# Decoder layer on one core: the up biases of the expert network move from products of their own into the last row of the up weights

## The chip, the cores and the metric

The kernel runs on one core of a Trainium2 chip. The metric is the device time of one execution in microseconds (us). The engines are called PE (TensorE, the matmuls), DVE (VectorE), ACT (ScalarE), POOL (GpSimd) and SP (SyncE, which here only issues transfers).

## What is computed

A decoder layer with three parts, each followed by a residual sum and a layer norm without gain or offset: self attention with circulant projections, cross attention to a context, and a mixture of 8 experts of which each token takes two, plus one shared expert. There are 16 batches of 128 tokens with 128 features. The change lies in the third part:

```
def _layernorm(x, axis=-1, eps=1e-05):
    m = jnp.mean(x, axis=axis, keepdims=True)
    v = jnp.var(x, axis=axis, keepdims=True)
    return (x - m) / jnp.sqrt(v + eps)
...
    x = _layernorm(x + _L0_xattn_ref(x, ctx_1024, ...), axis=-1)
    x = _layernorm(x + _L0_ffn_ref(x, ...), axis=-1)
...
        scores = jax.nn.softmax(xt @ gate_w.T, axis=-1)
...
            h = swiglu((xt @ ew1 + eb1) * (xt @ ew3 + eb3))
            return (acc + ce[:, None] * (h @ ew2 + eb2), None)
...
    shared = swiglu((xt @ sw1 + sb1) * (xt @ sw3 + sb3)) @ sw2 + sb2
```

The up weights `w1` and `w3` are 128 x 512 for each expert, the down weights `w2` 256 x 128. The input of the third part, called X2 in the kernel, is the output of a layer norm, so the 128 features of each of its rows sum to zero.

## The kernel before, in words

All engines run programs that are written out by hand and tied together by semaphores. The first two parts run in slots n = -20 to 72. There are four slots to a batch (`U = 4`); slot n holds attention step n of PE, ACT and DVE, and beside it the steps k = 1 to 8 of the chains of one to three earlier batches (`chain_steps`). Slots 0 to 63 begin on PE between 40 and 222 us. In step k = 1 and k = 7 of a chain DVE forms the statistics of a layer norm, POOL the reciprocal root (`root`, L612 and L614), and DVE then writes the normed rows X1 (L995) or X2 (L1004). POOL also adds a bias row before and after (X1B L652, XB L669), multiplies `hq_x` (L655), halves the down weights (L679, `HALVE_SLOTS`), and scatters the rows of X2 to their experts' places in DRAM (`xs`, L634), from slot 41 on. SP issues every load of weights, in slots given by the tables `BIAS_SLOTS`, `UP_SLOTS` and `DOWN_SLOTS`, between the loads of the attention parts, in program order: what stands ahead in SP's queue delays what stands behind. The up weights of experts 6 and 7 are loaded last, in slots 67 and 68, since their place holds other data until then.

From slot 66 on follow the tiles of the third part. Two groups of four batches take the shared expert in pieces between slots 25 and 63 (`shared`). All else is 47 tiles of 128 rows (m = 0 to 46): 8 of the shared expert, then 39 (`NR`) that are loaded from `xs` and take one expert each, whose number PE loads into a register (L1520). Step m of PE transposes the hidden rows `hid` of tile m-2 and the input rows of tile m+1 into pO (L1492, L1494), which ACT copies to `XH` (L852); it makes the two up products of tile m into pS and pT (L1501), and the down product of tile m-2 into pM (L1512). ACT copies pS (L858), DVE multiplies it with pT (L1071), clips it (L1073, L1074), ACT takes a tanh (L855), and DVE forms the gate and `hid` (L1076, L1079). ACT weights pM (L868) and POOL scatters it to `ys` (L712). Where PE waits for `hid` of tile m-2, a step is late by what DVE is late.

Each bias is added by a product of its own: three bf16 parts of all bias rows stand in the rows of `bias3`, nine rows of 128, and `bias_rows` picks three of them (L1502 into pS and pT, L1514 into pM). The three parts are made on POOL in slot 24 and pass through DRAM. The shared expert's early pieces add their biases on ACT and DVE instead, by column (`b1_col`, `b3_col`).

The tiles 8 to 23 come from rows that groups 0 to 2 have scattered. The last group's rows are scattered by POOL between the tiles (`LAST_SCATTER`), and SP waits for all of these scatters before it loads the rows of tile 24, whose transpose stands in step 23. Between tiles 5 and 17 DVE also works out the routing of the last group and the table of tiles (`LAST_ROUTING`, `LAST_TILES`).

Of the kernel before, what the change touches and what calls it, by code (L numbers as in the profile page):

```python
# [14 lines left out]
P = 128  # L15
B = 16
D = 128
# [20 lines left out]
BROWS = ((E + 1) * I2 // P, (E + 1) * I2 // P, (E + 1) * D // P)  # L38
# [8 lines left out]
BIAS_SLOTS = {7: 0, 11: 1, 15: 2}  # L47
# [6 lines left out]
XW = D + 2  # L54
# [7 lines left out]
UP_SLOTS = {**{15 + 4 * e: e for e in range(E - 2)}, 67: E - 2, 68: E - 1}  # L62
# [6 lines left out]
def decoder_layer(nc, x, ctx_1024, wq_c, wq_b, wk_c, wk_b, wv_c, wv_b, wo_c, wo_b, w_sim, b_sim, W_qv, b_qv,  # L69
# [3 lines left out]
    bias_scr = nc.dram_tensor("bias_scr", (3, sum(BROWS), P), BF16)  # L73
# [5 lines left out]
    with ctx:  # L79
# [13 lines left out]
        bias_rows = sb("bias_rows", [P, 3, P], BF16)  # L93
# [19 lines left out]
        gw_sb = sb("gw_sb", [E, D])  # L113
        gwT = sb("gwT", [P, E])
# [7 lines left out]
        bias_f = sb("bias_f", [sum(BROWS), P])  # L122
        bparts = sb("bparts", [sum(BROWS), 3, P], BF16)
        bias3 = sb("bias3", [P, (E + 1) * I2], BF16)
# [4 lines left out]
        X2T = sb("X2T", [P, 2, P])  # L129
        XT = sb("XT", [P, 2, G4 * P])  # L130
# [81 lines left out]
        XH = sb("XH", [P, 2, 3 * P])  # L212
# [6 lines left out]
        hidT = [hid[:].rearrange("p k n -> p (k n)"), W1[:, (E - 2) * I2:(E - 1) * I2]]  # L219
        b1_col, b3_col = sb("b1_col", [P, 2, 2]), sb("b3_col", [P, 2, 2])  # L220
        x2_of = [W[:, (E - 1) * I2:E * I2] for W in (W1, W3)]
        lin_g, lin_l = XH[:].rearrange("p k n -> p (k n)")[:, 0:G4 * P], PT[:, 3, :]
# [28 lines left out]
        s_bias3 = sem("s_bias3")  # L251
        s_w_shared, s_w_up, s_w_last, s_w_down = (sem(n) for n in ("s_w_shared", "s_w_up", "s_w_last", "s_w_down"))
        s_bcol = sem("s_bcol")
# [125 lines left out]
        def _(sp):  # L379
# [83 lines left out]
            def up_weights(e, done):  # L463
                a, c = (w1[e], w3[e]) if e < E else (sw1, sw3)
                sp.dma_start(W1[:, e * I2:(e + 1) * I2], a).then_inc(done, 16)
                sp.dma_start(W3[:, e * I2:(e + 1) * I2], c).then_inc(done, 16)
# [13 lines left out]
            for n in range(FIRST_SLOT, LAST_SLOT + 1):  # L480
# [16 lines left out]
                if n in BIAS_SLOTS:  # L497
                    k = BIAS_SLOTS[n]
                    routed, shared = ((b1, sb1), (b3, sb3), (b2, sb2))[k]
                    row = sum(BROWS[:k])  # L500
# [3 lines left out]
                if n == 21:  # L504
                    for to, src in ((b1_col, sb1), (b3_col, sb3)):
                        sp.dma_start(to[:], src.rearrange("(c p l) -> p c l", c=2, l=2)).then_inc(s_bcol, 16)
# [1104 lines left out]
```

## Time and profile before

| | |
|---|---|
| median of 3 runs | 418.36 us (418.06 to 418.45) |
| the profiled execution | 419.23 us, span 417.5 us |
| PE busy | 347.8 us (83% of the span) |
| DVE busy | 282.4 us (68%) |
| POOL busy | 195.5 us (47%) |
| ACT busy | 175.2 us (42%) |
| mean granted clock of PE | 0.956 |
| transfers | 39.56 MB |

The span is what the trace shows; the execution's own time has 1.7 us around it. Busy shares are means over a program with stages of different kinds, so they don't say which engine sets the end of a stage.

### The profile page before, as it was taken

Reading aid. Unit: us, or ns where it says so; the run is one execution under the profiler, and the core shown is the slowest. Engines: PE = TensorE matmul, PEld = TensorE weight load, DVE = VectorE, ACT = ScalarE, POOL = GpSimd, SP = SyncE. Lnnn points to the kernel's source line nnn. Section 1 sums busy time; section 2 is a strip of 40 time slices with the busy share of each in tenths; the row PEclk is TensorE's granted clock in tenths of the full one; section 3 lists DMA queues with packets and bytes.
Section 4 is the critical chain, followed back from the end, with each engine's and each line's share of the span. In section 5 each row is a group of like instructions: output and inputs, shape, how many; then the busy total and the mean of one; then the engine's idle time right before and its main releaser. Section 6 shows DMA issues by size and latency. Waiting matters only on the chain.

```text
span 417.5 us, 8518 instructions
## 1 busy us (share of the span) xinstructions
PE 347.8 (83%) x2415; PEld 224.0 (54%) x2415; DVE 282.4 (68%) x834; ACT 175.2 (42%) x498; POOL 195.5 (47%) x377
## 2 busy tenths in 40 slices
PE   2637887887998987878978699899999999999790
PEld 1223465665765666556657455455456555555450
DVE  3345477776669887888886866788866666666232
ACT  2122344443443452435452154345555555555313
POOL 9700022224213258753275534346888665656223
PEclk9999999998888999989998699999999999999897
DMA  4774644766726533220002100111322111110063
GB/s 98 172 207 123 196 143 117 209 197 175 207 75 206 156 110 91 64 74 23 23 28 72 63 19 26 40 32 52 90 61 64 54 44 46 45 40 19 27 203 100
DMA packets 53197, 39.56 MB, mean 95 GB/s; under 512 B 7623, under 2 KB 46632, under 8 KB 53147
## 3 DMA queue, kind: packets, MB, share of 16 engines
q1 hardware_dynamic: 50881, 34.33, 29.8%
q0 software_dynamic: 2272, 4.69, 3.4%
q8 instruction: 22, 0.36, 0.4%
q14 instruction: 22, 0.18, 0.1%
HBM read 26.05 MB, written 12.69 MB: 93 GB/s over the span
## 4 chain that ended last, share of the span: by engine, by line
PE 50%; DVE 19%; issue 8%; DMA 7%; POOL 7%; SPq 6%; ACT 2%; ACTq 0%; POOLq 0%; DVEq 0%
PE pT L1501 9%; PE pS L1501 9%; PE pM L1512 5%; DVE negmax L934 3%; PE pO L1492 3%; PE pM L1307 2%; DVE inv_den L950 2%; PE pT L1502 2%; PE pS L1502 2%; PE pT L1478 2%; POOL rstd L614 2%; POOL xs L634 2%; PE pO L1344 2%; PE pT L1331 2%; PE pS L1321 2%
## 5 line engine op out<-in xcount | busy, mean ns | idle before, releaser
L712 POOL DMA_INDIRECT ys<-sim_rhs,row_dest x39 | 40.5, 1038 | 36.7 <-ACT sim_rhs L868 32.8
L766 ACT ACTIVATE PT<-pT 128x512 f32<-128x512 f32 x64 | 38.0, 593 | 36.5 <-PE pT L1331 36.1
L1501 PE MATMUL pT<-W,XH 128*128 (+1 forms) x94 | 50.5, 619 | 0.0
L934 DVE TENSOR_REDUCE negmax<-pS 128x4 f32<-128x512 f32 x64 | 43.4, 679 | 9.0 <-PE pS L1321 8.7
L1501 PE MATMUL pS<-W,XH 128*128 (+1 forms) x94 | 49.0, 604 | 0.0
L612 POOL TENSOR_SCALAR vareps<-meanvar 128x1 f32<-128x1 f32 x32 | 8.5, 264 | 86.6 <-DVE meanvar L963 86.3
L1321 PE MATMUL pS<-Kdiag,Qst 128*128 128x512 f32 x64 | 41.5, 655 | 4.9 <-DMA Kdiag<-parts_scr 4.1
L1071 DVE TENSOR_TENSOR PT<-pT,PT 128x512 f32<-128x512 f32 x47 | 32.4, 690 | 19.4 <-PE pT L1502 16.3
L852 ACT COPY XH<-pO 128x384 f32<-128x384 f32 x47 | 22.5, 479 | 46.6 <-PE pO L1494 39.9
L1512 PEld LDWEIGHTS pM<-W,XH 128*128 128x128 f32 x188 | 28.5, 194 | 18.1 <-issue 14.4
L634 POOL DMA_INDIRECT xs<-X,slot x32 | 33.5, 1048 | 7.5 <-issue 5.2
L1331 PE MATMUL pT<-Qdiag,Kst 128*128 128x512 f32 x64 | 30.8, 482 | 2.6 <-DMA Qdiag<-maxT 2.2
L1512 PE MATMUL pM<-W,XH 128*128 (+1 forms) x188 | 29.4, 279 | 1.3 <-ACT XH L852 1.3
L655 POOL TENSOR_TENSOR hq_x<-X1T,hqT 128x128 f32<-128x128 f32 x16 | 7.3, 456 | 49.0 <-ACT hqT L787 49.0
L1076 DVE SCALAR_TENSOR_TENSOR Vz<-Vz,XT 128x256 f32<-128x256 f32 x47 | 20.1, 427 | 14.1 <-ACT Vz L855 12.5
L858 ACT COPY PT<-pS 128x512 f32<-128x512 f32 x47 | 27.2, 580 | 2.4 <-PE pS L1502 2.2
L855 ACT ACTIVATE Vz<-XT 128x256 f32<-128x256 f32 x47 | 19.6, 417 | 19.4 <-DVE XT L1073 17.2
L1344 PE MATMUL pO<-PT,Vz 128*32 128x128 f32 x512 | 27.6, 289 | 0.0
L1348 PE MATMUL pO<-PT,head_ones 128*32 128x128 f32 x512 | 26.5, 280 | 0.0
L1492 PEld LDWEIGHTS pO<-ident,hid 128*128 128x128 f32 x94 | 12.2, 142 | 23.3 <-issue 16.7
L1492 PE MATMUL pO<-ident,hid 128*128 128x128 f32 x94 | 18.4, 277 | 4.5 <-issue 1.7
L1478 PE MATMUL pT<-W 128*128 128x512 f32 x32 | 21.0, 743 | 0.7 <-DVE XH L1043 0.7
(264 smaller groups left out, 823.6 us busy)
## 6 DMA issues: line engine op xcount, KB each, us to landing
parts_scr<-qk_hi SPq DMA_DIRECT2D x16, 256.0 KB, 3.1
W<-in_L_ffn_w SPq DMA_DIRECT2D x16, 256.0 KB, 4.0
Qst<-parts_scr SPq DMA_DIRECT2D x32, 96.0 KB
Kdiag<-parts_scr SPq DMA_DIRECT2D x64, 48.0 KB
Kst<-parts_scr SPq DMA_DIRECT2D x32, 96.0 KB
Qdiag<-parts_scr SPq DMA_DIRECT2D x64, 48.0 KB
sim_add<-xs SPq DMA_DIRECT2D x39, 65.0 KB
parts_scr<-qk_lo SPq DMA_DIRECT2D x8, 256.0 KB, 3.4
```

Of the source, the lines that this page charges most:

```text
L634: pool.indirect_dma_start(xs.ap(), bass.IndirectOffsetOnAxis(ap=slot[:, k, b:b + 1], axis=0), X2[:, b, :], None).then_inc(scat_sem(g), 16)
L712: pool.indirect_dma_start(ys.ap(), bass.IndirectOffsetOnAxis(ap=row_dest[:, k:k + 1], axis=0), YO[:, i % RING, :], None).then_inc(s_ysc[i ...
L766: act.activation(PT[:, u % 3, :], pT[:, 0, :], ACT.Exp, scale=SCALE).then_inc(p_sb, 1)
L934: dve.tensor_reduce(out=negmax[:, b % 2, HG * j:HG * (j + 1)], in_=pS[:, u % 2, :].rearrange("p (g k) -> p g k", g=HG), axis=AX.X, op=ALU.max,
L1071: dve.tensor_tensor(prod[:, p, :], pT[:, p, :], up1[:, p, :], ALU.mult).then_inc(prod_sb, 1)
L1321: pe.matmul(pS[:, u % 2, :], Qst[:, (b // 2) % 2, j, (b % 2) * P:(b % 2 + 1) * P], Kdiag[:, b % 2, j, :, :], start=True, stop=True).then_i ...
L1331: pe.matmul(pT[:, 0, :], Kst[:, (b // 2) % 2, j, (b % 2) * P:(b % 2 + 1) * P], Qdiag[:, b % 2, j, :, :], start=True, stop=True).then_inc(s ...
L1344: pe.matmul(pO[32 * hg:32 * hg + 32, 0:P], Vz[:, b % 2, hg, j, :], PT[:, u % 3, hg * P:(hg + 1) * P], start=(j == 0), stop=(j == U - 1), s ...
L1478: pe.matmul(pT[:, 1, :], (W1, W3)[step % 2][:, first:first + 2 * P - step // 2:2], x2_of[g], start=True, stop=True).then_inc(f_ps, 1)
L1492: mm = pe.transpose(pO[:, k * P:(k + 1) * P], hid[:, p, k * P:(k + 1) * P], ident[:])
L1501: pe.matmul(bank, XH[:, 1 - p, 2 * P:3 * P], W[:, bass.ds(e_up * I2, I2)], start=True, stop=False)
L1512: pe.matmul(pM[:, 0:D], XH[:, p, k * P:(k + 1) * P], W2[:, bass.ds(e_y * I + k * D, D)], start=(k == 0), stop=False)
```

## The change

Because each row of X2 sums to zero, its feature 0 is minus the sum of the others. So x @ W is the sum over the features 1 to 127 of x_d (W_d - W_0), which needs only 127 rows, and the 128th row of the contraction is free: X2 gets a column of ones behind its features, the transposes take columns 1 to 128 of it, and the bias is the last row of the weights. What the diff does:

- For each of the nine experts SP now issues four loads in place of two: rows 1 to 126 of each up weight to 126 partitions, and row 0 broadcast to 128 partitions (`first_rows_of`). Row 127 and the bias of all experts come in eight loads in slot 11 (`up_biases`). The slots are 13 for the shared expert and 21 + 5e for expert e, and each waits until the subtractions of the one before are done (`w_less`).
- POOL subtracts the broadcast row from each up weight, 127 x 512, 18 in all, in the third and fourth slot behind each load (`LESS_SLOTS`: 16, 17, 24, 25, 29, 30, 34, 35, 39, 40, 44, 45, 49, 50, 54, 55, 59, 60).
- The two bias products of each tile's up products go. The bias product of the down product stays, with three partitions in place of 128, and moves ahead of the second up product; the down product moves behind it.
- The gate weights get the same treatment by one small subtraction on DVE; the bias parts of the down product are made of 9 rows instead of 81 and no longer pass through DRAM; POOL's clearing of `bias3` and the making of `bias_rows` go.
- The shared expert's early pieces need no bias on ACT and DVE; some buffers that lay in the weights get their own place, so that experts 6 and 7 load in slots 51 and 56.
- The rows of `xs` have 131 elements instead of 130.

```
-UP_SLOTS = {**{15 + 4 * e: e for e in range(E - 2)}, 67: E - 2, 68: E - 1}
+UP_SLOTS = {13: E, **{21 + 5 * e: e for e in range(E)}}
+LESS_SLOTS = {n + 3 + k: (e, k) for n, e in UP_SLOTS.items() for k in range(2)}
...
+                i = LESS_ORDER[e]
+                if i:
+                    sp.wait_ge(w_less, 2 * i)
+                for k, (W, w) in enumerate(((W1, w1 if e < E else sw1), (W3, w3 if e < E else sw3))):
+                    first = e * D * I2 if e < E else 0
+                    sp.dma_start(W[0:P - 2, e * I2:(e + 1) * I2],
+                                 bass.AP(w.tensor, first + I2, [[I2, P - 2], [1, I2]])).then_inc(s_w_up, 16)
+                    sp.dma_start(first_rows_of[:, k, :], bass.AP(w.tensor, first, [[0, P], [1, I2]])).then_inc(s_w_up, 16)
...
+                if n in LESS_SLOTS:
+
+                    e, k = LESS_SLOTS[n]
+                    here = (W1, W3)[k][0:P - 1, e * I2:(e + 1) * I2]
+                    pool.wait_ge(s_w_up, 64 * (LESS_ORDER[e] + 1))
+                    pool.wait_ge(s_w_bias, 128)
+                    pool.tensor_tensor(here, here, first_rows_of[0:P - 1, k, :], ALU.subtract).then_inc(w_less, 1)
...
-                    pe.matmul(bank, XH[:, 1 - p, 2 * P:3 * P], W[:, bass.ds(e_up * I2, I2)], start=True, stop=False)
-                    pe.matmul(bank, bias_rows[:, k, :], bias3[:, bass.ds(e_up * I2, I2)], start=False,
+                    pe.matmul(bank, XH[:, 1 - p, 2 * P:3 * P], W[:, bass.ds(e_up * I2, I2)], start=True,
                               stop=True).then_inc(done, 1)
...
+                if y:
+
+                    if m >= 3:
+                        pe.wait_ge(y_sb, m - 2)
+                    pe.matmul(pM[:, 0:D], three[:], b2_parts[:, bass.ds(e_y * D, D)], start=True, stop=False)
+                if up:
+                    product(pT[:, p, :], W3, b_ps, prod_sb)
                 if y:
                     pe.wait_ge(xh_sb, m + 2)
-                    if m >= 3:
-                        pe.wait_ge(y_sb, m - 2)
                     for k in range(2):
-                        pe.matmul(pM[:, 0:D], XH[:, p, k * P:(k + 1) * P], W2[:, bass.ds(e_y * I + k * D, D)],
-                                  start=(k == 0), stop=False)
-                    pe.matmul(pM[:, 0:D], bias_rows[:, 2, :], bias3[:, bass.ds(e_y * D, D)], start=False,
-                              stop=True).then_inc(y_ps, 1)
-                if up:
-                    product(pT[:, p, :], W3, 1, b_ps, prod_sb)
+                        mm = pe.matmul(pM[:, 0:D], XH[:, p, k * P:(k + 1) * P], W2[:, bass.ds(e_y * I + k * D, D)],
+                                       start=False, stop=(k == 1))
+                    mm.then_inc(y_ps, 1)
```

PE's program for one tile of an expert, before (ISA and REGISTER_ALU rows set addresses from the expert's number):

```order
L1520 TENSOR_LOAD expert_of
L1520 ISA x2
L1492 MATMUL pO<-ident,hid 128x128 x2
L1494 MATMUL pO<-ident,sim_add 128x128
L1501 MATMUL pS<-W1,XH 128x512
L1502 MATMUL pS<-bias3,bias_rows 128x512
L1512 MATMUL pM<-W2,XH 128x128
L1514 MATMUL pM<-bias3,bias_rows 128x128
L1501 REGISTER_ALU
L1501 MATMUL pT<-W3,XH 128x512
L1502 MATMUL pT<-bias3,bias_rows 128x512
```

The same tile now (`XH` is part of the buffer `first_rows_of`, whose name stands in its place):

```order
L1526 TENSOR_LOAD expert_of
L1526 ISA x2
L1497 MATMUL pO<-ident,hid 128x128 x2
L1499 MATMUL pO<-ident,sim_add 128x128
L1506 MATMUL pS<-W1,first_rows_of 128x512
L1515 MATMUL pM<-b2_parts,three 128x128
L1506 REGISTER_ALU
L1506 MATMUL pT<-W3,first_rows_of 128x512
L1521 MATMUL pM<-W2,first_rows_of 128x128
```

Two products of 512 columns are gone, and the down product stands last.

POOL's program in slots 44 to 46, before:

```order
L634 DMA xs<-X2,slot 17536x130
L669 TENSOR_TENSOR XB<-X,bo_row 128x128
L655 TENSOR_TENSOR hq_x<-X1T,hqT 128x128
L612 TENSOR_SCALAR vareps<-meanvar 128x1
L614 TENSOR_TENSOR rstd<-vareps,neg_half 128x1
L624 COPY X2<-dest 128x4
L625 COPY X2<-weight 128x4
L652 TENSOR_TENSOR X1B<-X1,bqv_row 128x128
```

and now:

```order
L666 TENSOR_TENSOR XB<-X,bo_row 128x128
L676 TENSOR_TENSOR W1<-W1,first_rows_of 127x512
L652 TENSOR_TENSOR hq_x<-X1T,hqT 128x128
L609 TENSOR_SCALAR vareps<-meanvar 128x1
L611 TENSOR_TENSOR rstd<-vareps,neg_half 128x1
L621 COPY X2<-dest 128x4
L622 COPY X2<-weight 128x4
L631 DMA xs<-X2,slot 17536x131
L676 TENSOR_TENSOR W3<-W3,first_rows_of 127x512
L649 TENSOR_TENSOR X1B<-X1,bqv_row 128x128
```

The two subtractions L676 stand between the work for the chains and the scatters.

SP's queue around slots 11 to 14 now (before, the first eight rows were two loads to `bias_f`, and the four of slot 13 were two loads of 128 x 512):

```order
L480 DMA W1<-in_L0_ffn_w1 1x8x512
L482 DMA W1<-in_L0_ffn_sw1 1x512
L483 DMA W1<-in_L0_ffn_b1 1x4096
L484 DMA W1<-in_L0_ffn_sb1 1x512
L452 DMA Qdiag<-parts_scr 24x4x128 x4
L461 DMA Qdiag<-maxT 1x16x128 x2
L522 DMA xs<-pad_row 128x131
L487 DMA W2<-in_L0_ffn_sw2 128x2x128
L472 DMA W1<-in_L0_ffn_sw1 126x512
L474 DMA first_rows_of<-in_L0_ffn_sw1 128x512
L472 DMA W3<-in_L0_ffn_sw3 126x512
L442 DMA Kdiag<-parts_scr 24x4x128 x4
```

Six more issues stand ahead of slot 12's loads, and two more ahead of slot 14's `Kdiag`.

## Rows read from the trace of the kernel before

**Rows 1.** Busy time by stretch: us, then PE, PEld, DVE, ACT, POOL, PEclk, DMA share, GB/s

```profile
77.00:101.00 24.00, 19.27 (x217) 14.13 (x220) 18.85 (x59) 10.19 (x37) 9.21 (x22) 1.00 0.74 211
101.00:158.00 57.00, 52.51 (x497) 37.46 (x487) 44.73 (x144) 25.03 (x84) 18.12 (x37) 0.88 0.51 148
158.00:241.00 83.00, 66.76 (x638) 49.44 (x627) 66.94 (x227) 31.30 (x110) 47.44 (x79) 0.92 0.18 55
...
263.00:300.00 37.00, 35.15 (x159) 19.48 (x160) 30.65 (x98) 17.75 (x44) 21.56 (x44) 1.00 0.20 52
...
315.10:387.80 72.70, 72.70 (x336) 42.64 (x335) 49.27 (x120) 40.65 (x96) 45.53 (x93) 1.00 0.16 43
```

**Rows 2.** Timeline of PE: step 23's start, and one later step in full

```profile
315.14 0.38 PE L1492 MATMUL pO<-ident,hid 128*128 128x128 f32 x2
...
333.35 0.38 PE L1492 MATMUL pO<-ident,hid 128*128 128x128 f32 x2
...
333.67 1.02 PE L1501 MATMUL pS<-W,XH 128*128 x2
...
334.53 0.38 PE L1502 MATMUL pS<-bias,bias_rows 128*128 x1
...
334.75 0.61 PE L1512 MATMUL pM<-W,XH 128*128 x4
...
335.19 0.22 PE L1514 MATMUL pM<-bias,bias_rows 128*128 x1
...
335.25 1.08 PE L1501 MATMUL pT<-W,XH 128*128 x2
...
336.16 0.38 PE L1502 MATMUL pT<-bias,bias_rows 128*128 x1
```

**Rows 3.** Timeline of DVE and ACT in the same step

```profile
333.55 0.69 DVE L1071 TENSOR_TENSOR PT<-pT,PT 128x512 f32<-128x512 f32 x1 [0.65 <-PE pT L1502]
...
333.87 0.48 ACT L852 COPY XH<-pO 128x384 f32<-128x384 f32 x1 [1.09 <-PE pO L1494]
...
334.60 0.42 ACT L855 ACTIVATE Vz<-XT 128x256 f32<-128x256 f32 x1 [0.25 <-DVE XT L1073]
...
335.45 0.37 ACT L868 ACTIVATE sim_rhs<-pM,row_weight 128x128 f32<-128x128 f32 x1
335.51 0.42 DVE L1079 SCALAR_TENSOR_TENSOR hid<-XT,Vz 128x256 f32<-128x256 f32 x1
```

**Rows 4.** Chain of work that ended last, at step 7

```profile
257.57 2.35 DMA xs<-X,slot
...
262.92 0.44 PE pO L1492 x2
```

**Rows 5.** Timeline of POOL at four places

```profile
178.35 1.19 POOL L642 TENSOR_TENSOR X<-X 128x512 f32<-128x512 f32 x1
...
266.93 1.18 POOL L642 TENSOR_TENSOR X<-X 128x512 f32<-128x512 f32 x1
...
286.49 1.06 POOL L712 DMA_INDIRECT ys<-sim_rhs,row_dest  x1 [0.84 <-ACT sim_rhs L868]
...
309.12 1.00 POOL L634 DMA_INDIRECT xs<-X,slot  x1 [0.17 <-issue]
```

**Rows 6.** Timeline of SP's queue at slots 11 to 15

```profile
68.23 0.36 SPq L502 DMA_DIRECT2D bias_f<-in_L_ffn_b  x1
...
73.75 0.43 SPq L465 DMA_DIRECT2D W<-in_L_ffn_sw  x1
...
77.02 1.20 SPq L407 DMA_DIRECT2D parts_scr<-qk_hi  x2
```

**Rows 7.** Section 6 of the page, DMA issues: KB each, us to landing

```profile
W<-in_L_ffn_w SPq DMA_DIRECT2D x16, 256.0 KB, 4.0
```

**Rows 8.** Timeline of DVE at the two POOL instructions L642

```profile
177.64 1.99 DVE L1004 TENSOR_SCALAR X<-R,meanvar,rstd 128x128 f32<-128x128 f32 x1
...
266.99 1.27 DVE L1073 TENSOR_SCALAR XT<-PT 128x256 f32<-128x256 f32 x1
268.18 0.28 DVE L1074 TENSOR_SCALAR XT<-PT 128x256 f32<-128x256 f32 x1
```

More of the change, by code:

```diff
@@ L218, in decoder_layer @@
         hid = sb("hid", [P, 2, I])
[L219 to L222, printed above, removed]
+        hid_b = sb("hid_b", [P, G4 * P])
+        hidT = [hid[:].rearrange("p k n -> p (k n)"), hid_b[:]]
+        x2T_g = sb("x2T_g", [P, SG, G4 * P])
+        x2_of = [x2T_g[:, g, :] for g in range(SG)]
+        lin_g, lin_l = sb("lin_g", [P, G4 * P])[:], PT[:, 3, :]
         YO = sim_rhs[:].rearrange("p b j -> p (b j)")[:, 0:RING * D].rearrange("p (r x) -> p r x", r=RING)
@@ L519, in _ @@
                     sp.wait_ge(bias_step, 5)
-                    sp.dma_start(bias_scr.ap().rearrange("t r n -> r t n"), bparts[:]).then_inc(s_biasw, 16)
-                if n == 34:
-                    sp.wait_ge(s_biasw, 16)
-                    sp.wait_ge(c_bias, 1)
-                    row = 0
-                    for k, rows in enumerate(BROWS):
-                        sp.dma_start(bias3[3 * k:3 * k + 3, 0:rows * P],
-                                     bias_scr.ap()[:, row:row + rows, :].rearrange("t r n -> t (r n)")).then_inc(s_bias3, 16)
-                        row += rows
+                    for part in range(3):
+                        sp.dma_start(b2_parts[part:part + 1, :].rearrange("p (e n) -> p e n", n=D),
+                                     bparts[:, part, :]).then_inc(s_biasw, 16)
             sp.wait_ge(s_scat, 16 * 2 * G4 * (NG - 1))
@@ L802, in shared_up @@
                 elif step == 0:
-                    if g == 0 and c == 0:
-                        act.wait_ge(s_bcol, 32)
-                    else:
+                    if g or c:
                         act.wait_ge(f_hid, 2 * g + c)
                     act.wait_ge(f_ps, done + 1)
-                    act.activation(lin_g, pT[:, 1, :], ACT.Identity, bias=b1_col[:, c, 0:1], scale=1.0).then_inc(f_out, 1)
+                    act.copy(lin_g, pT[:, 1, :]).then_inc(f_out, 1)
                 elif step == 2:
@@ L814, in shared_up @@
                     act.wait_ge(f_ps, done + 1)
-                    act.activation(lin_l, pT[:, 1, :], ACT.Identity, bias=b1_col[:, c, 1:2], scale=1.0).then_inc(f_out, 1)
+                    act.copy(lin_l, pT[:, 1, :]).then_inc(f_out, 1)
             def copy_logits(b):
@@ L889, in _ @@
                         route_exp(g)
+                if n == FFN_SLOT - 1:
+                    act.wait_ge(w_less, 2 * (E + 1))
                 if n >= FFN_SLOT - 1:
@@ L1456, in shared @@
                 if g == 0 and i == 0:
-                    pe.wait_ge(s_w_shared, 48)
+                    pe.wait_ge(w_less, 2 * (LESS_ORDER[E] + 1))
+                    pe.wait_ge(s_w_bias, 128)
                 if g or i:
@@ L1472, in shared @@
                                       stop=False)
-                        mm = pe.matmul(here, bias_rows[:, 2, :], bias3[:, E * D:(E + 1) * D], start=False, stop=True)
+                        mm = pe.matmul(here, three[:], b2_parts[:, E * D:(E + 1) * D], start=False, stop=True)
                     mm.then_inc(f_ps, 1)
```

114 lines of the change are left out of this document (50 added, 64 removed).

## The prediction

> **What bounds the kernel now.** I read the busy times by stretch first [rows 1]. From 315.1 to 387.8 us PE is busy for all of 72.7 us at a granted clock of 1.00: nothing but PE's own instructions sets the pace there. From 263 to 300 it is busy for 35.2 of 37 us, and DVE for 30.7. In the slots it is different. From 101 to 158 PE has 52.5 of 57 us (92%), and from 158 to 241 neither PE (66.8 of 83) nor DVE (66.9) is full: there the chains between DVE, POOL and PE set the end. From 77 to 101 PE has only 19.3 of 24 us while the transfers have their highest share, 0.74.
>
> Then I read one step of PE [rows 2]. It begins with the transposes at 333.35, and the transposes of the next follow the last bias product, which begins at 336.16, by 0.21 us, at 336.38: the step is 3.03 us. The starts give what each instruction holds PE for: the product into pS 0.86 (333.67 to 334.53), its bias 0.22 (to 334.75), the down product 0.44, its bias 0.06, the product into pT 0.91, its bias about 0.22. (The durations shown are longer, since an instruction's end overlaps its successor.)
>
> **The third part.** Without the two bias products a step is 3.03 - 0.43 = 2.60 us on PE, if nobody makes PE wait. DVE's work on a tile begins at 333.55, 0.21 after the bias product's last column is issued, and `hid` ends 335.51 + 0.42 = 335.93, so 2.38 us later [rows 3]. Now pT is ready one down product earlier: DVE begins 0.45 - 0.21 = 0.24 us before the next step starts. On ACT the weighting of pM (0.37) now falls at 0.2 us into the step, ahead of the XH copy (0.48), which so ends near 1.0; the tanh, ready at 0.8 (it starts 1.05 after DVE's first instruction now), waits until then. `hid` then ends near 2.31, where PE's first weight load of the next step wants it by about 2.40. That is tight but holds; I take 2.62 for the step, 0.41 less than now.
>
> This gain isn't had at every tile. Four terms, in order of time:
>
> 1. Up to step 7. The chain from slot 66 to the last scatter of group 2 holds four up bias products, 4 x 0.22 = 0.9 us. From that scatter to PE's step 7 it is 262.92 - 257.57 = 5.35 us [rows 4] of transfers, which stay.
> 2. Steps 7 to 17. DVE gets its first product earlier by the down product and the bias, about 0.9 us, and by a little in the wait for `hid`. After that DVE itself is the bound, since it also does the last routing (30.7 of 37 us busy), and a shorter step on PE gives nothing.
> 3. Steps 18 to 22 shorten, but step 23 waits for the rows of tile 24, and these for the last scatter. It begins at 309.12 [rows 5]; with the 5.35 us of step 7 the rows are there at 314.5, and step 23 begins now at 315.14 [rows 2], so only 0.7 us behind. POOL has been busy without a gap since the scatter of tile 11's result at 286.49 [rows 5], which comes earlier by term 1 and by about 0.4 (ACT's weighting is earlier only by what the steps gain less what the down product moves back). So step 23 can begin earlier by 0.9 + 0.4 + 0.7 = 2.0 us. This is all that the first 23 steps give.
> 4. From step 23 to step 47 there are 24 steps: 24 x 0.41 = 9.8 us. At the end the last tile's work on DVE begins one down product earlier: 0.5 us.
>
> Sum: 2.0 + 9.8 + 0.5 = 12.3 us less. Bounds: 24 x 0.43 + 2.8 = 13 at best, or a little more if the scatters come sooner; 8 if a step stays at 2.8.
>
> **The slots.** First SP. In slots 11 and 13 it has eight more issues, at 0.36 to 0.43 each [rows 6], 3.2 us. It is busy without a gap there, and the chain goes through it from the spill at 77.02. But it has eight fewer in slots 15, 19 and 23 and in the bias columns of slot 21, and two more in slot 21, so that by slot 24 it is 2 issues behind, 0.9 us. The bytes are about even up to there (experts 1 and 2 come later, the broadcast rows are added). Against the 0.9 stands that the maxima's small transfer of slot 21 no longer queues behind a pair of weights. From slot 26 on the load has 1 MB a time instead of 0.5; a weight lands 4.0 us after its issue [rows 7], and two or three slots of about 3 us lie between load and use. The new wait for `w_less` holds SP's queue, with the loads of the attention parts behind it, until POOL's subtraction in the slot before; it ends before SP gets there in the slots that I followed. I take 0.5 us, between -1 and +3. What else is new costs nothing: DVE's subtraction for the gate weights stands beside loads that PE waits for anyway, at worst 0.3 us; POOL's cleared start (5 us less) was hidden by the same loads.
>
> The Trainium skill (DMA: Bandwidth & Descriptors, "Why a DMA increments its semaphore by 16 and not by 1") says that a transfer uses the largest number of engines up to 16 that divides its partitions, so 126 partitions take 14 and 127 would take one. By it, as an estimate, the 4.0 us would be 4.6, still inside the slots between; no run here shows a load of 126 partitions yet.
>
> Then the 18 subtractions. POOL has one instruction of the same kind, two inputs of 128 x 512: 1.19 us [rows 5]. So POOL gets 18 x 1.19 = 21.4 us more, in 17 to 240 us of which it is idle for more than half. The time is not free, for two reasons. POOL is in order, and a subtraction stands ahead of a root or a scatter. And DVE is stopped beside it: L1004 of 177.64 takes 1.99 us and ends as POOL's L642 of 178.35 ends; L1073 of 266.99 takes 1.27, beside the 0.28 of L1074 behind it, under the L642 of 266.93 [rows 5, 8]. That is 0.98 us lost for a 1.18 us instruction. A subtraction behind a root begins just when DVE wants to write X1 or X2 from it, so it meets this nearly always.
>
> What the path sees of it is bounded by 0 below and 18 x 0.98 = 17.6 us above (21.4 if POOL's whole time counted). Ten stand in slots 16 to 40, up to 158 us, where PE is 92% busy or SP sets the pace: there X1 is mostly there before PE comes to its transpose, and I count two in full, 2 us. Eight stand in slots 44 to 60, where DVE, POOL and PE wait for each other by turns, the two of slots 44 and 45 between scatters on a full POOL. There I count half of POOL's time, 8 x 0.6 = 4.8 us. With SP's 0.5 that makes 7.3, say 7 us more.
>
> **The sum**: the profiled execution took 419.2 us; 419.2 - 12.3 + 7.0 = 413.9. It is 0.9 above the median of the runs, so I expect **413.0** there.
>
> **Rivals.** *The subtractions are covered.* POOL is idle for 35 of the 83 us from 158 to 241, and a chain that comes late may find its successor late anyway. If the slots lose only 1.5 us, the result is 419.2 - 12.3 + 1.5 - 0.9 = 407.5. Against it speak the two DVE rows, both of which met the instruction in the worst moment.
>
> *The stop of DVE is paid every time*, and this is the one that ends slower. Each subtraction takes 0.98 us from DVE, which is 81% busy from 158 us on, and the next X1 or X2 is late by that. 419.2 - 12.3 + 17.6 + 0.5 - 0.9 = 424.1. It decides from 12.3 / 18 = 0.68 us a subtraction on. For it speaks that PE's wait for X1 is in line with everything behind; against it, the 92% of PE up to 158 us.
>
> The Trainium skill (SBUF — State Buffer, "Who interferes with whom") says that DVE with two SBUF inputs or in its two-port mode and a GpSimd instruction that reads SBUF exclude each other, the second waiting for the whole of the first. The rows agree, with 0.98 of 1.18 us; by the whole instruction the last sum would be about 428.
>
> *The steps don't shorten as far*: the tanh behind the XH copy, or POOL's stretched small work (it has 45.5 of 72.7 us and would have the same in 63), holds a step at 2.8 us. Then term 4 is 24 x 0.23 = 5.5 and the result 413.0 + 4.3 = 417.3. That would be the change not doing what it is for. PE alone can't be the reason.
>
> **How the numbers follow.** I give my forecast 0.50 (its own range 409 to 417), the covered subtractions 0.26 (404 to 409), the stop paid every time 0.16 (419 to 426), steps of 2.8 us 0.08 (415 to 420). A measurement of this kernel tells about 0.2%, 0.8 us, from no change. Faster is then nearly all of the first, all of the second and a third of the last: 0.77; same 0.07; slower 0.16. The range from 404.5 to 421 leaves out the lowest of the second and the upper half of the third.
>
> **What the profile would show.** Right: the starts of the transposes 2.6 us apart from step 23 on, with PE full at clock 1.00; a gap on PE of 1 to 2 us ahead of step 23, ended by the load; DVE back to back from step 8 to 17; 18 instructions of POOL near 1.2 us, with L1004 and its like at over 1.2 us beside them; the end of slot 63 some 7 us later than now. Wrong: a step of more than 2.7 us; slots that end within 2 us of now, or more than 12 us later; PE waiting at slots 14 to 18 for `Kdiag` or `Qdiag` rows behind the 1 MB of slot 13, which I priced at nearly nothing.

## The result, and the profile after

The changed kernel takes 437.4 us (median of four runs, 434.4 to 438.1), the kernel before 418.2 beside it: 1.046 times as long, 95% interval 1.042 to 1.050. The profiled execution took 438.1 us with a span of 436.3 us; the span before was 417.5. I had forecast 413.0 and no more than 421.

The busy times by stretch come first (us, then PE, PEld, DVE, ACT, POOL, granted clock, DMA share, GB/s). The stretches run from the start of slot 16 to that of 19, from there to 40, and to 63:

```profile
79.40:95.60 16.20, 10.75 (x93) 8.05 (x93) 7.87 (x21) 4.54 (x16) 5.40 (x9) 0.68 0.67 190
95.60:162.80 67.20, 56.30 (x529) 40.86 (x528) 53.62 (x159) 27.37 (x92) 28.93 (x52) 0.92 0.66 172
162.80:246.50 83.70, 67.58 (x614) 49.59 (x613) 68.67 (x192) 29.12 (x103) 52.92 (x79) 0.83 0.34 94
```

The same three stretches of the kernel before:

```profile
77.60:86.90 9.30, 7.87 (x94) 5.62 (x93) 6.80 (x21) 4.33 (x16) 2.90 (x7) 1.00 0.80 234
86.90:151.80 64.90, 57.83 (x528) 41.27 (x528) 50.36 (x159) 27.79 (x92) 21.59 (x46) 0.89 0.57 163
151.80:222.00 70.20, 57.63 (x613) 42.44 (x612) 58.91 (x192) 29.43 (x103) 40.49 (x69) 0.97 0.19 53
```

The same instructions of PE take 6.9 us longer in three slots, 2.3 longer in the next 21, and 13.5 longer in the last 23. With 1.8 us up to slot 16, slot 63 starts 24.5 us later (246.5 against 222.0). I had forecast 7. The granted clock, the last column but two, tells a second thing: it is 0.68 and 0.83 in the first and the last stretch, where it was 1.00 and 0.97. Up to 380 us PE's stretches at 1.2 GHz add up to 61 us, before to 27. In slots 40 to 63 PE is busy for 67.6 us with the products that took it 57.6, so 10 of the 13.5 us are the same instructions running longer, and the rest is idle time.

The third part gave back 5.7 of these 24.5 us, not 12.3. A step is 2.85 us, not 2.62: from step 23 to step 47 it is 68.2 us where it was 72.7. One step on PE, and the weight loads of the down bias and of the product behind it, which answer to [rows 2]:

```profile
359.07 0.38 PE L1497 MATMUL pO<-ident,hid 128*128 128x128 f32 x2
...
359.40 1.02 PE L1506 MATMUL pS<-W,first_rows_of 128*128 x2
...
360.35 0.09 PEld L1515 LDWEIGHTS pM<-b_parts,three 3*128 3x128 bf16 x1 [0.76 <-issue]
360.35 0.23 PE L1515 MATMUL pM<-b_parts,three 3*128 x1
...
360.51 0.30 PEld L1506 LDWEIGHTS pT<-W,first_rows_of 128*128 128x128 f32 x2
360.51 1.13 PE L1506 MATMUL pT<-W,first_rows_of 128*128 x2
...
361.47 0.61 PE L1521 MATMUL pM<-W,first_rows_of 128*128 x4
...
361.91 0.38 PE L1497 MATMUL pO<-ident,hid 128*128 128x128 f32 x2
```

From start to start: pS holds PE for 0.95 us (0.86 before), the down bias for 0.16 (0.06), pT for 0.96. The weights of the down bias, 3 partitions, are loaded at 360.35, at the start of their product and not ahead of it.

In the slots two places tell how the time goes. The first is slot 17, on SP, PE and POOL:

```profile
78.53 0.37 SPq L474 DMA_DIRECT2D first_rows_of<-in_L_ffn_sw  x1
79.00 2.41 SPq L442 DMA_DIRECT2D Kdiag<-parts_scr  x4
...
85.96 1.27 POOL L676 TENSOR_TENSOR W<-W,first_rows_of 127x512 f32<-127x512 f32 x1 [5.02 <-DMA first_rows_of<-in_L_ffn_sw]
86.79 0.77 PE L1325 MATMUL pS<-Kdiag,Qst 128*128 128x512 f32 x1 [4.83 <-issue]
```

SP issues `Kdiag`, the keys, at 79.00 behind the large loads (75.23 before; here the eight bias loads also stand ahead). The trace doesn't show when they land; the product that reads them starts only at 86.79. PE is idle for 4.8 us, and afterwards this product takes 0.77 us, the granted clock from 85 to 90 being 0.50. The second place is slots 49 and 50:

```profile
201.83 1.25 POOL L676 TENSOR_TENSOR W<-W,first_rows_of 127x512 f32<-127x512 f32 x1
201.88 1.29 DVE L1001 TENSOR_SCALAR X<-R,meanvar,rstd 128x128 f32<-128x128 f32 x1 [1.00 <-POOL rstd L611]
...
203.22 0.33 PE L1396 MATMUL pX<-ident,X 128*128 128x128 f32 x1 [1.61 <-DVE X L1001]
...
203.66 1.26 POOL L676 TENSOR_TENSOR W<-W,first_rows_of 127x512 f32<-127x512 f32 x1
203.69 1.39 DVE L989 SCALAR_TENSOR_TENSOR wx<-wqv,hc 128x128 f32<-128x128 f32 x1
...
205.13 0.80 PE L1417 MATMUL pX<-wx,X1T 128*128 128x128 f32 x2 [1.34 <-DVE wx L989]
```

Two subtractions, two instructions of DVE that take 1.29 and 1.39 us where their like take 0.35 and 0.34, and each time PE waits for just this one. The granted clock of the stretch with the first wait, and of the one behind it:

```profile
200.90:204.30 3.40, 1.28 (x30) 0.70 (x19) 2.42 (x3) 0.98 (x5) 3.08 (x5) 0.96 0.14 42
204.30:208.00 3.70, 2.87 (x12) 2.77 (x13) 1.89 (x5) 1.16 (x3) 0.85 (x2) 0.50 0.44 131
```

PE was busy for 1.3 of 3.4 us, and runs the next 3.7 at 1.2 GHz.

### The profile page after: what moved, and what is told of

It is laid out like the page before. It is cut to its first block, busy times and chain, and to the rows that moved or that the text cites. A ratio compares the mean times of both kernels' runs of the same rounds, so it can differ in the third digit from the quotient of the medians.

```text
span 436.3 us, 8297 instructions
## 1 busy us (share of the span) xinstructions
PE 351.0 (80%) x2321; PEld 222.9 (51%) x2321; DVE 296.6 (68%) x836; ACT 176.0 (40%) x498; POOL 212.4 (49%) x393
## 4 chain that ended last, share of the span: by engine, by line
PE 51%; DVE 22%; issue 10%; DMA 6%; POOL 5%; SPq 4%; ACT 2%; ACTq 0%; POOLq 0%; DVEq 0%
PE pT L1506 11%; PE pS L1506 9%; PE pM L1521 5%; DVE negmax L940 4%; PE pM L1311 3%; PE pO L1497 3%; DVE inv_den L956 2%; POOL rstd L611 2%; PE pT L1335 2%; PE pS L1325 2%; PE pO L1348 2%; DMA X<-in_x 2%; PE pM L1515 2%; PE pO L1352 1%; DVE stats L967 1%
## 5 line engine op out<-in xcount | busy, mean ns | idle before, releaser
L1506 PE MATMUL pT<-W,first_rows_of 128*128 (+1 forms) x94 | 53.5, 651 | 0.0
L1325 PE MATMUL pS<-Kdiag,Qst 128*128 128x512 f32 x64 | 42.9, 677 | 11.6 <-issue 7.8
L1506 PE MATMUL pS<-W,first_rows_of 128*128 (+1 forms) x94 | 49.7, 612 | 0.0
L609 POOL TENSOR_SCALAR vareps<-meanvar 128x1 f32<-128x1 f32 x32 | 8.5, 267 | 83.6 <-DVE meanvar L969 83.4
L1521 PEld LDWEIGHTS pM<-W,first_rows_of 128*128 128x128 f32 x188 | 28.2, 191 | 22.4 <-issue 22.4
L1335 PE MATMUL pT<-Qdiag,Kst 128*128 128x512 f32 x64 | 32.5, 508 | 1.7 <-DMA Qdiag<-maxT 1.4
L1521 PE MATMUL pM<-W,first_rows_of 128*128 (+1 forms) x188 | 28.8, 275 | 0.6 <-ACT first_rows_of L856 0.5
L872 ACT ACTIVATE sim_rhs<-pM,row_weight 128x128 f32<-128x128 f32 x39 | 14.3, 367 | 34.6 <-PE pM L1521 32.3
L1352 PE MATMUL pO<-PT,head_ones 128*32 128x128 f32 x512 | 28.2, 296 | 0.0
L676 POOL TENSOR_TENSOR W<-W,first_rows_of 127x512 f32<-127x512 f32 x18 | 22.9, 1270 | 8.4 <-DMA first_rows_of<-in_L_ffn_sw 5.0
L856 ACT COPY first_rows_of<-pO 128x384 f32<-128x384 f32 x47 | 22.5, 478 | 8.7 <-PE pO L1499 7.9
L1325 PEld LDWEIGHTS pS<-Kdiag,Qst 128*128 128x128 f32 x64 | 14.8, 234 | 19.6 <-issue 19.4
```

The costliest lines, as they stand in the source:

```text
L1325: pe.matmul(pS[:, u % 2, :], Qst[:, (b // 2) % 2, j, (b % 2) * P:(b % 2 + 1) * P], Kdiag[:, b % 2, j, :, :], start=True, stop=True).then_i ...
L1335: pe.matmul(pT[:, 0, :], Kst[:, (b // 2) % 2, j, (b % 2) * P:(b % 2 + 1) * P], Qdiag[:, b % 2, j, :, :], start=True, stop=True).then_inc(s ...
L1352: mm = pe.matmul(pO[32 * hg:32 * hg + 32, P:2 * P], head_ones[:, j, :], PT[:, u % 3, hg * P:(hg + 1) * P], start=False, stop=(j == U - 1), ...
L1506: pe.matmul(bank, XH[:, 1 - p, 2 * P:3 * P], W[:, bass.ds(e_up * I2, I2)], start=True, stop=True).then_inc(done, 1)
L1521: mm = pe.matmul(pM[:, 0:D], XH[:, p, k * P:(k + 1) * P], W2[:, bass.ds(e_y * I + k * D, D)], start=False, stop=(k == 1))
```

## The experiments

Chips differ a little (the kernel before takes 415.9 to 418.4 us on them), so each result is given as a ratio to the kernel before on the same chip, with its 95% interval. Slots are timed by the start of their product into pT (L1335). As slot 0 starts up to 1.9 us earlier in one trace than in another, the length of slots 40 to 63 is given beside the place where they end: it is 83.6 us in the changed kernel and 70.2 before. Slot times come from one trace of each kernel. How far they scatter is seen in the first run below, which leaves the slots' work as it is: 14.5 us in place of 16.2 in slots 16 to 19, 83.0 in place of 83.6 in slots 40 to 63, and slot 63 at 246.2 in place of 246.5.

**The down bias product with 128 partitions**

```
-        three = sb("three", [3, P], BF16)
+        three = sb("three", [P, P], BF16)
...
-        b2_parts = sb("b2_parts", [3, (E + 1) * D], BF16)
+        b2_parts = sb("b2_parts", [P, (E + 1) * D], BF16)
...
+            pool.memset(b2_parts[:], 0.0).then_inc(c_bias, 1)
```

> The changed kernel (437.4), with one edit: the weights and the bias rows of the down bias product have 128 partitions, of which all but three bias rows are zero, in place of 3. After the change a step of the third part is 2.85 us, and the weight load of this product starts together with the product (360.35), 0.76 us after the load before it, while the load of the old kernel's bias products stood behind the running product. Theory A (a weight load of 3 partitions is not taken ahead of a running product of 128): the step falls to 2.62, 24 steps and most of the earlier ones give 5 to 9 us, 429 to 432. Theory B (it is the place of this product between the two large ones, not its size): 2.85 and 437 as before.

Ratio 1.032 (1.025 to 1.039), 430.0 us. The weights are now loaded while the product ahead of them still runs, and a step is 2.60 us:

```profile
385.18 1.02 PE L1508 MATMUL pS<-W,first_rows_of 128*128 x2
...
385.62 0.10 PEld L1517 LDWEIGHTS pM<-b_parts,three 128*128 128x128 bf16 x1 [0.24 <-issue]
...
386.05 0.22 PE L1517 MATMUL pM<-b_parts,three 128*128 x1
386.10 0.65 PE L1508 MATMUL pT<-W,first_rows_of 128*128 x1
```

This is theory A: it is the size of the product, not its place. From step 23 to 47 it is 62.4 us in place of 68.2. From slot 63 to step 23 only 0.9 us are gained (91.8 in place of 92.7).

**Subtractions on one column**

```
-                    pool.tensor_tensor(here, here, first_rows_of[0:P - 1, k, :], ALU.subtract).then_inc(w_less, 1)
+                    pool.tensor_tensor(here[:, 0:1], here[:, 0:1], first_rows_of[0:P - 1, k, 0:1], ALU.subtract).then_inc(w_less, 1)
```

> The changed kernel (437.4), but the 18 subtractions of GpSimd are done on one column of 512 only, so the up weights are not made right; all loads and waits stay. The 18 instructions take 1.27 us each now. Theory P (the slots lose their time to these subtractions, through VectorE's stop and GpSimd's queue): slot 63 ends 10 us or more earlier, about 425. Theory T (they lose it to the transfers): only the rise in slots 43 to 61 shrinks, by 2 to 5 us, and the 8.8 us that are lost by slot 19 stay; 433 to 436.

Ratio 1.014 (1.009 to 1.019), 422.7 us; slot 63 starts at 232.2, 14.3 us earlier, and slots 40 to 63 take 69.5 us, 14.1 less. But slot 40 starts at 162.7, where it did in the changed kernel (162.8). So both theories hold, each for its stretch. Eight subtractions run before PE begins slot 40, and they cost nothing that lasts. Ten begin behind it, since POOL comes to those of slots 39 and 40 only at 163.0 and 165.7, and they cost 1.4 us each. Of the 8.8 us that are lost by slot 19, 7.4 are still lost here, so that is something else. PE's time at 1.2 GHz falls from 61 to 31 us.

**The first row to one partition**

```
-    sp.dma_start(first_rows_of[:, k, :], bass.AP(w.tensor, first, [[0, P], [1, I2]])).then_inc(s_w_up, 16)
+    sp.dma_start(first_rows_of[0:1, k, :], bass.AP(w.tensor, first, [[0, 1], [1, I2]])).then_inc(s_w_up, 16)
```

> The changed kernel (437.4), but the row that is taken off is loaded to one partition (2 KB) and not to all 128 (256 KB); GpSimd subtracts zeros elsewhere, so the up weights are not made right. 18 transfers of 256 KB, 4.7 MB, are gone. Theory T (bytes in the way of the attention parts): the wait of 4.83 us for the keys of slot 17 shrinks to under 3, and the slots end 5 to 12 us earlier, 425 to 432. Theory P (the subtractions): 0 to 2 us, 435 to 437. Theory I (SP's issues, which are as many as before): under 3 us.

Ratio 1.044 (1.037 to 1.050). No theory was met in full: theory T had 5 to 12 us at the end of the slots. PE's wait of 4.8 us ahead of slot 17 is gone, and slots 16 to 19 take 11.0 us in place of 16.2 (9.2 before). But slot 16 starts 2.0 us later, for a reason that no run shows, and slots 19 and 63 are both 3.2 us earlier. The bytes count at slot 17.

**The bias loads in slot -4**

```
+EARLY_BIAS = -4
...
-                if n == 11:
+                if n == EARLY_BIAS:
                     up_biases()
```

> The changed kernel (437.4), with the eight small loads of the biases and last rows in slot -4, where SP waits 2.4 us for the maxima, in place of slot 11, where they take SP 3.7 us out of a queue without gaps. Theory I (issues): slot 17 starts some 3 us earlier and the end of the slots too, 433 to 435. Theory T (only the bytes of slot 13 count): SP's time comes back in its wait for these bytes, 436 to 438.

Ratio 1.038 (1.030 to 1.046), an interval that overlaps that of the changed kernel. The trace is of an execution of 439.2 us, where the other three took 430.8 to 435.8, so where its slots end says nothing on this edit. Its slots 16 to 19 take 13.4 us, 1.0 less than in the run with the down bias alone. By itself this edit leaves open whether SP's issues count; a closer comparison follows with the mends together.

**The third part alone**

```
-                    pe.matmul(bank, bias_rows[:, k, :], bias3[:, bass.ds(e_up * I2, I2)], start=False,
...
```

This is an edit of the kernel before. In the rest of it, not shown, the down bias product stands between the up products and the down products behind them.

> The kernel before with the third part of the change alone: its two up bias products are left out (so the up biases are missing from the output), the down bias product stands between the up products and still has 128 partitions, the down products stand behind. No load and no subtraction is new. Theory D (the gain of 12.3 us that was forecast for this part is there when the slots don't change): step 2.60 us from step 23 on, 405 to 407. Theory L (the transfers and DVE hold the tiles anyway): over 409.

Ratio 0.972 (0.966 to 0.977), 405.8 us beside 417.5: theory D, the forecast gain is there. A step is 2.60 us. Against the trace before, step 23 comes 1.3 us earlier, step 47 11.6, and the end 13.2.

**Two powers in place of a subtraction**

```
-                    pool.tensor_tensor(here, here, first_rows_of[0:P - 1, k, :], ALU.subtract).then_inc(w_less, 1)
+                    for i in range(2):
+                        at = 4 * LESS_ORDER[e] + 2 * k + i
+                        last = pool.tensor_tensor(idle_pow[:, at:at + 1], neg_half[:], neg_half[:], ALU.pow)
+                    last.then_inc(w_less, 1)
```

> The changed kernel (437.4; 435 beside a kernel before of 415.9), but each of the 18 subtractions is replaced by two powers of one column, 2 x 0.56 us on GpSimd, which hold GpSimd's queue for nearly as long (1.12 of 1.27 us) and read next to nothing of SBUF; the up weights are not made right. With the subtractions on one column, slot 63 came 14.3 us earlier. Theory V (the loss is VectorE's stop beside an instruction of GpSimd that reads much of SBUF): VectorE's instructions beside them take 0.3 us and not 1.3, and it ends within 2 us of the kernel with one column, 421 to 425. Theory Q (the loss is GpSimd's queue, with the root behind the subtraction): 432 to 435.

Ratio 1.020 (1.014 to 1.026), 426.0 us; slots 40 to 63 take 72.4 us, which is 11.2 of the 14.1. The same place as above, slot 49:

```profile
197.35 1.06 POOL L679 TENSOR_TENSOR idle_pow<-neg_half 128x1 f32<-128x1 f32 x2
197.40 0.35 DVE L1005 TENSOR_SCALAR X<-R,meanvar,rstd 128x128 f32<-128x128 f32 x1 [1.00 <-POOL rstd L612]
```

POOL is held as long as before but for 0.2 us, and DVE takes 0.35. By excess I mean what DVE's instructions take beside those of POOL over the median of their like. Beside the 36 powers it is some 0.3 us in all, where it was 14.7 beside the 18 subtractions. This is theory V, the stop of VectorE. The 2.9 us that slots 40 to 63 take longer here than with subtractions on one column are what GpSimd's queue is worth of the 14.1.

**Quarters**

```
-                    pool.tensor_tensor(here, here, first_rows_of[0:P - 1, k, :], ALU.subtract).then_inc(w_less, 1)
+                    for q in range(4):
+                        part = slice(q * P, (q + 1) * P)
+                        last = pool.tensor_tensor(here[:, part], here[:, part], first_rows_of[0:P - 1, k, part], ALU.subtract)
+                    last.then_inc(w_less, 1)
```

> The changed kernel (435 beside 415.9), but each subtraction is made in four instructions of 128 columns in place of one of 512; the result is the same. Theory V with a stop that ends with the instruction: VectorE waits for one quarter, 0.3 us, not for 1.3; the slots from 44 on lose 2 to 6 us in place of 14, 424 to 431. If GpSimd's next quarter goes ahead of the waiting VectorE, the stop stays 1.3 us or gets longer: 435 to 438. Theory Q: 435 or more, as four instructions take longer than one.

Ratio 1.033 (1.026 to 1.039); slots 40 to 63 take 76.3 us, 7.3 less, about half of what leaving the subtractions out gives:

```profile
198.41 1.70 POOL L678 TENSOR_TENSOR W<-W,first_rows_of 127x128 f32<-127x128 f32 x4
198.47 0.48 DVE L1004 TENSOR_SCALAR X<-R,meanvar,rstd 128x128 f32<-128x128 f32 x1 [1.00 <-POOL rstd L611]
```

Here DVE is stopped by one quarter (0.43 us) and not by all four. GpSimd pays 0.43 us more for each subtraction. It doesn't always go so. Beside the last of the 18, DVE begins while POOL's scatter still runs, and is let go only behind the fourth quarter, with 2.29 us for an instruction that takes 0.28:

```profile
230.78 2.29 DVE L1214 SCALAR_TENSOR_TENSOR biased<-pick,biased 128x32 f32<-128x32 f32 x1
...
231.32 1.69 POOL L678 TENSOR_TENSOR W<-W,first_rows_of 127x128 f32<-127x128 f32 x4
```

So the rival, GpSimd's next quarter going ahead of the waiting VectorE, came true too, once in this run.

**The large loads later**

```
-UP_SLOTS = {13: E, **{21 + 5 * e: e for e in range(E)}}
+UP_SLOTS = {18: E, **{24 + 5 * e: e for e in range(E)}}
```

> The changed kernel (435 beside 415.9), but the shared expert's four large loads stand in slot 18 and not in slot 13, and those of the experts three slots later each (24, 29, ... 59). Theory T (the 1 MB of slot 13 is in the way of the keys of slots 14 to 17): the wait of 4.8 us ahead of slot 17 goes, slot 19 starts 5 us earlier or more, and if the gain stays, 428 to 431. Theory I (only the eight bias loads of slot 11 count): slot 19 within 2 us of the changed kernel, 433 to 436. The subtractions now meet other work, which can move the end by 3 us either way.

Ratio 1.036 (1.029 to 1.044). Slot 17 starts at 81.4, 3.4 us after slot 16, as it did before the change; it was 8.0. Slots 16 to 19 take 11.8 us in place of 16.2. Slot 63 starts 3.6 us earlier, 1.4 of it from before slot 16. Theory T holds for slot 17: without the 1 MB ahead of the keys the wait is gone, though the eight bias loads are where they were. For the end of the kernel I had expected 428 to 431 us, and it is 434.3.

**All mends together, in four forms.** Common to them are 128 partitions for the down bias and the bias loads in slot -4. The first has quarters and the later loads; the second has the later loads and whole subtractions on DVE:

```
+                if n in LESS_SLOTS:
...
+                    dve.wait_ge(s_w_up, 64 * (LESS_ORDER[e] + 1))
...
+                    dve.tensor_tensor(here, here, first_rows_of[0:P - 1, k, :], ALU.subtract).then_inc(w_less, 1)
```

The third and the fourth put both subtractions of an expert on GpSimd behind the sum for XB, whole and in quarters:

```
+UP_SLOTS = {17: E, **{25 + 4 * e: e for e in range(E)}}
+LESS_SLOTS = {n + 3: ((e, 0), (e, 1)) for n, e in UP_SLOTS.items()}
```

> The full computation, with four mends of the changed kernel together: the down bias product with 128 partitions, the eight bias loads in slot -4, the large loads in slots 18, 24, ... 59, and each subtraction in four instructions of 128 columns. If the single gains add (to the end of the slots: 7.7 for the quarters, 3.6 for the loads, near 0 for the biases; and 0.24 a step from step 23 on, 6), it takes 417 us less than nothing over the kernel before: 416 to 421 beside a kernel before of 416.5, so within 1%. If VectorE's stops and the keys' transfers cause the same idle time of PE, the gains overlap: 422 to 426.

> The full computation; as the one before, but the subtractions are whole and made by VectorE, at the end of its work of the same slot. VectorE gets 18 x 0.7 us more work and GpSimd none; nobody is stopped by a long instruction of GpSimd. Theory V gives 8 x 0.7 = 5.6 us on a path that VectorE is on about half the time, so 3 us in place of 14: 413 to 418. If VectorE waits there for the loads, slots 24 to 60 end later by some us at each of them: 420 or more.

> The full computation; down bias product with 128 partitions and bias loads in slot -4 as above, and both subtractions of an expert, whole (1.27 us each), stand together in a slot 20, 28, 32, ... 56, behind GpSimd's sum for XB; there GpSimd then waits 3 to 4 us for ScalarE's hqT, and of five subtractions in such slots of the changed kernel only the ones beside the routing met VectorE. Theory V: it is the place that decides; few stops of VectorE, the slots end 8 to 14 us before the changed kernel's, 414 to 421. Theory Q' (2.5 us in one piece are too long for GpSimd's queue, hq_x comes late): 424 or more.

> The full computation; as the one before, with each subtraction in four instructions. GpSimd's work in such a slot is 3.4 us in place of 2.5, which is all of its idle time there; VectorE's stops get shorter. If the stops matter more: 1 to 3 us less than the one before. If GpSimd's queue does: 1 to 4 us more.

| | ratio | 95% interval | us | slot 63 |
|---|---|---|---|---|
| quarters | 1.004 | 1.000 to 1.007 | 419.3 | 234.5 |
| on DVE | 0.989 | 0.984 to 0.994 | 413.4 | 228.4 |
| both in one slot, whole | 1.029 | 1.024 to 1.034 | 430.3 | 245.8 |
| both in one slot, quarters | 1.015 | 1.008 to 1.022 | 424.9 | 240.7 |

The gains of the first add up at slot 63: it is 12.0 us earlier, where quarters and later loads alone gave 7.7 and 3.6. They don't by stretch. Slots 40 to 63 take 81.3 us here and took 76.3 with quarters alone, so the price of a subtraction depends on what it meets there. Up to slot 19 this form differs from the one with later loads only in the place of the bias loads: slots 16 to 19 take 9.2 us in place of 11.8, but slot 16 starts 1.9 us later, so that slot 19 gains 0.7.

The subtractions on DVE make the one version of the whole computation that beats both kernels, by 1.1% over the one before: 0.68 us of DVE each (0.82 in the mean) in place of a stop of 1.0 at a moment that it can't choose. The third was my error: I had picked the place because DVE wasn't met there in most cases, and it was met in eight of nine. The worst case:

```profile
195.68 3.62 DVE L1008 TENSOR_SCALAR A<-Aexp,Ainv 128x120 f32<-128x120 f32 x1
...
196.75 2.48 POOL L677 TENSOR_TENSOR W<-W,first_rows_of 127x512 f32<-127x512 f32 x2
...
199.36 0.57 PE L1405 MATMUL pX<-ident,A 128*121 128x128 f32 x1 [4.58 <-DVE negmax L941]
```

DVE's instruction, which takes 0.3 us alone, begins under POOL's scatter (195.32), is held on through the sum for XB and through both subtractions, and PE waits 4.6 us. In the fourth form the same place is no better. DVE is let go only behind the seventh of the eight quarters:

```profile
193.05 4.07 DVE L1011 TENSOR_SCALAR A<-Aexp,Ainv 128x120 f32<-128x120 f32 x1
...
194.11 3.34 POOL L679 TENSOR_TENSOR W<-W,first_rows_of 127x128 f32<-127x128 f32 x8
...
197.17 0.50 PE L1408 MATMUL pX<-ident,A 128*121 128x128 f32 x1 [4.62 <-DVE negmax L944]
```

In both kernels instructions of POOL that follow each other closely held a waiting DVE over several of them. Which waiting instruction is let in between two quarters and which isn't, no run settles.

**Only the 18 subtractions, in the kernel before**

```
+LESS_SLOTS = (16, 17, 24, 25, 29, 30, 34, 35, 39, 40, 44, 45, 49, 50, 54, 55, 59, 60)
...
+                if n in LESS_SLOTS:
+                    here = spare_w[0:P - 1, :]
+                    pool.wait_ge(spare_less, 1 + LESS_SLOTS.index(n))
+                    pool.tensor_tensor(here, here, here, ALU.subtract).then_inc(spare_less, 1)
```

> The kernel before, the full computation, and nothing changed but 18 subtractions of 127x512 on GpSimd, on a spare tile, at the places where the changed kernel has its own. Theory V plus clock (each of the last eight costs the slots 1.8 us, of which 1.0 is VectorE's stop and the rest PE's lower clock behind it, the first ten next to nothing): 12 to 17 us more than before, 429 to 434 beside 417.5. If the price of 14 us came only about together with the late transfers, so that the parts don't add: under 8 us more.

Ratio 1.030 (1.024 to 1.035), 430.9 us. Slot 19 starts 3.1 us later than before, slot 40 only 1.2, slot 63 13.1; slots 40 to 63 take 82.1 us, 11.9 more. An instruction takes 1.04 us here, and most stops are 0.7 to 0.8 us; the price of the ten behind the start of slot 40 is 1.2 us each. So the price is there without any new load.

**Everything taken out**

> The changed kernel with everything mended or left out that has cost time so far: subtractions on one column, the first row loaded to one partition, the large loads later, the bias loads in slot -4, the down bias product with 128 partitions (the up weights are not made right). If these are all causes of the loss, the slots end within 2 us of the kernel before (222.0), and it takes what the third part alone took: ratio 0.97, 405 to 408. If a cause is missing (the wait of SP for w_less, the 126 partitions, the missing aliases): 409 or more.

Ratio 0.967 (0.962 to 0.972), 405.3 us. Slot 19 starts at 88.5, slot 40 at 150.6 and slot 63 at 221.8 (before: 86.9, 151.8, 222.0). The ratio is that of the third part alone within the intervals, so no cause is missing: loads of 126 partitions, the wait for `w_less` and the separate buffers cost nothing that can be seen. The Trainium skill (DMA: Bandwidth & Descriptors, "Why a DMA increments its semaphore by 16 and not by 1") would give such a load 14 engines; by this run it makes no difference to the whole.

## Why the prediction was wrong, point by point

Three steps failed. In the profiled spans the result is 23.8 us above the forecast. The term of SP and its transfers was 9.7 us too small (0.5 forecast, 10.2 measured), that of the subtractions 7.5 (6.8 forecast, 14.3 measured), and the third part gave 6.6 less than forecast (12.3, measured 5.7). The signs that I had named for being wrong came, too: a step over 2.7 us, slots that end more than 12 us later, and PE waiting for `Kdiag`.

**"There I count half of POOL's time, 8 x 0.6 = 4.8 us"** (term of the subtractions). The step that failed is this weighing by halves. I had 2 us for the first ten and 4.8 for the last eight. The eight before PE's slot 40 cost nothing that lasts, and the ten behind its start cost 14.1 us, 1.4 each. The mechanism was the one of the second rival, DVE's stop at the worst moment: nine of these ten met an instruction of DVE, with some 10 us of excess in all. Its bound for the whole, 17.6 us, held against 14.3. Its price of 0.98 us for one did not hold everywhere: two of the ten have an excess of 1.8 us, where DVE was caught already under the scatter of POOL that stands ahead.

What makes 14.1 us out of 10 is open in part. Two powers, which hold the queue without stops, keep 2.9 us, and 1.3 are left. The stops make PE idle, and its granted clock in these slots is 0.83, against 0.98 without subtractions; PE's own instructions are busy 10 us longer for it. These times overlap, and no run separates the clock from the stops. What the runs have on the clock points both ways. In the run with the third part alone the clock of these slots is 0.92 in place of 0.97 and they take 70.6 us in place of 70.2, so a lower clock needn't cost time. But in the first of the four forms, with quarters, DVE's excess is 6 us, the clock is 0.83, and these slots take 81.3 us.

The Trainium skill (SBUF — State Buffer, "Who interferes with whom") calls the port that DVE and GpSimd share an exclusive lock, held for the whole instruction. Stops of 0.94 us under 1.25, and of 0.13 under a quarter of 0.43, agree. The powers, which read SBUF too, stopped nobody for a time that shows, and the stops through several quarters don't follow from one lock for one instruction. I had this rule in hand and gave the sum by it (428), and then weighed it by halves.

**"I take 0.5 us, between -1 and +3"** (SP's term). Measured, what isn't subtraction is 10.2 us at slot 63, 7.4 of them there by slot 19. I had followed SP's count of issues but priced the bytes at nothing: "The bytes are about even up to there" is right for the sum to slot 24 and wrong for slot 13, where 1 MB stands in one piece ahead of the keys, at a DMA share that was 0.74 already [rows 1]. The sign that I had named, PE waiting at slots 14 to 18 for `Kdiag` behind the 1 MB, came at slot 17 with 4.8 us. Of the 6.9 us that slots 16 to 19 take longer, moving the large loads took 4.4 away and that wait altogether, and moving the bias loads besides took the other 2.5, of which 1.9 came back as a later slot 16.

**"I take 2.62 for the step"**. This is right as a chain: with 128 partitions a step is 2.60 us, so DVE and ACT keep up. It is wrong for the kernel as written, 2.85. The step that failed is the down bias product's 0.06 us, which I took from rows of a product with 128 partitions [rows 2], and the new one has 3. It cost 24 x 0.24 = 5.8 us. The Trainium skill (TensorEngine Tiling (Array Packing), "Key Properties") says that changing the tiling mode drains TensorE. If a product of 3 partitions is issued as a smaller tile, that is a change and a change back in each step; the trace shows the lost time on both sides of the product, not the mode.

**The sum of the third part** stands for the product with 128 partitions: 12.3 forecast, 13.2 in the profiled spans and 11.7 between the medians. Term 4 was 10.3 (9.8 forecast), what comes before step 23 1.3 (2.0), the tail 1.6 (0.5).

**The rest.** The wait for `w_less` and the loads of 126 partitions cost nothing, as I had said. Of the rivals, the covered subtractions hold for the first eight. A step held at 2.8 us came out in size, but for a cause that I had ruled out: "PE alone can't be the reason". It was PE alone. Open is where the 6.4 us go by which slot 63 is still late in the best version: 1.9 of them are there by slot 16, and 4.5 come in slots 40 to 63, where DVE makes nine of its 18 subtractions (14.7 us for all).

## What to carry to other kernels

A long GpSimd instruction that reads SBUF can stop VectorE for as long as it lasts. On a path where PE waits for VectorE, count the stop in full at each meeting, and expect somewhat more than its sum: here 14.1 us of time for 10 of stops. Pieces let VectorE in mostly, but not every time. The same work on VectorE, where it is short, was the best form here. Look at a load not by its sum over the program but by what is queued right behind it. And a small matmul is priced by its own shape: keep zero rows in it if its neighbours use all 128 partitions.

## What the runs showed of the hardware that I had not expected

A bf16 product with 3 partitions between products with 128 costs 0.24 us more per step than the same with 128, 125 of them zero. An instruction of 127x512 on GpSimd in four pieces takes 1.70 us in place of 1.27. VectorE mostly gets in between the pieces, but in the run with quarters alone it was held through four of them once (2.29 us in place of 0.28) and, in the fourth form, through seven and through all eight. Not every instruction of VectorE is stopped: in the changed kernel one that reads PSUM (`pM`, L924) takes its usual 0.75 us right under a subtraction. All five stretches at 1.2 GHz in slots 40 to 63 of the changed kernel, 3.4 to 10.2 us long, began in or behind idle times of PE of 1.1 us or more; no run tests whether the idle time is what brings them.
